# Causal mask by 43 more contraction rows in the diagonal tiles, with the steps reordered

## The chip, the core and the metric

The kernel runs on one core of a Trainium2 chip. The core has five engines that run their own instruction streams: TensorE (PE, whose weight loads are listed apart as PEld), VectorE (DVE), ScalarE (ACT), GpSimd (POOL) and SyncE (SP), which here only issues DMAs. Sixteen DMA engines move the data; one DMA instruction is cut into packets that some of these engines carry. Engines wait for each other by semaphores; a DMA adds 16 to its semaphore in all. The metric is the device time of one execution in microseconds, as the median of several runs.

## The reference

Eight sequences of 512 tokens with 128 features go through layer norm, a gated linear attention with 8 heads and two decay states each, a sign-weight feed-forward layer, a causal attention with 16 heads of 8 features (rotary positions), and the same feed-forward layer again, each with a residual. All work on the change lies in the causal attention:

```
qkv = layernorm(x) @ qkv_w.T + qkv_b ; q, k get rotary positions      # 16 heads of 8
scores[q, k] = q . k / sqrt(8), for k <= q only
ctx = softmax(scores) @ v ; x = x + ctx @ proj_w.T + proj_b
```

## The kernel before

**Stages.** For each sequence b there are five stages: norm (letter n), scan (s, the linear attention), mid (m, the feed-forward and the projections for q, k, v), maxima (x) and attn (a). Each engine has its own generator for each stage, which yields between steps, and a string of letters for each engine (`PE_ORDER`, `ACT_ORDER`, `DVE_ORDER`, `POOL_ORDER`, `SP_ORDER`, lines 86 to 127) says whose next step comes. `interleave` walks through the string when the program is built, so each engine's instruction stream is fixed and in order: where one instruction waits, all behind it wait. Different sequences overlap: scan of sequence b+1 stands among maxima and attn of b.

**Operands of the attention.** Sixteen heads are handled in two sets of eight; f = 2b or 2b+1 counts the 16 sets. The queries and keys are each written as a sum of three bf16 parts (`parts`). SP writes the six part tiles of a sequence to DRAM (`scratch`, line 452: 128 rows of 1 KB each, the "spill"), waits until all six have landed (line 457), and then reads them back stacked, so that one contraction over 72 rows gives all nine products of parts (line 463). One such stack is five DMAs for `qs` and three for `ks`: four of 24 rows, two of 16 and two of 8, each row 8 KB. There are three places (`RING`) for stacks.

**Maxima** (PE line 1021): for each head and each of four query tiles of 128, scores against all keys up to and including the tile's own, 128 to 512 columns in one matmul over 72 rows, and then a second matmul (line 1023) of the bf16 identity with a tile of zeros and -3e38 that adds the mask on the 128 columns of the tile's own keys. Two tiles of heads by queries fill one PSUM bank of 512 columns, at 1, 1, 2 or 4 heads a group, 22 groups a set; DVE reduces a bank to row maxima (line 1491). Until the last sequence there is one bank for it. The negated maxima go in three bf16 parts, turned over by PE (line 1029) and copied by ACT (`mT`, line 749), by three small DMAs (line 472) into rows 72 to 74 of `qs`; rows 72 to 74 of `ks` are ones, written once by three DMAs at the start (line 435).

**Attention** (PE line 1051): the transposed scores, keys by queries, over 75 rows, so that the maximum is already subtracted; again a second matmul (line 1053) adds the mask on the diagonal tile. ACT takes the exponent of a bank (line 762), PE multiplies with the values (line 1066). Per set and head there are four tiles with a mask in each of the two passes, so there are 512 mask matmuls at each of the lines 1023 and 1053.

**SP's order.** It begins `nnmmmmmmmm`: after the loads at the start, the load of x for sequence 1, that for sequence 2 (line 425, which waits until the normalised x of sequence 1 has been taken), then the six spills of sequence 0 and its two stacks.

Of the kernel before, what the change touches and what calls it, by code (L numbers as in the profile page):

```python
# [15 lines left out]
P = 128  # L16
# [48 lines left out]
N_STACK = 16 * (len(Q_COPIES) + len(K_COPIES))  # L65
# [26 lines left out]
    "aaxsamaxasamaaxaasasaaamaaxasxaaamaxsaxaaxasaxsasxaxasxaxaaaxasxmaxsxamxsaaaaxsmxaasxaaaxsaaxsxasxsasxsa"
    "xssmxsaxsxasxasxsxasxassxaasxsxaassxsaxaaaxsaaxsxaasxasxaaaxaamxasaxaaaxmasaxaaxaaxsaxaaasxaamxaxaasxama"
    "xaaxsaxsxaxasxasaxsxaasxasxaaxasasxaaxaasxmaxassaxmaxasxsmxasxsasxsaxmxsaxsxaxasaxsaxasxaaxasasaxssaxsxa"
    "sxsaxsaxaaasaxsaaxssaaamasxamxsxaaxaaxaaxaaaxsaaxsxaxaamxasxaaaxaaxasxaaaxsaaxmxaxsassaxaaxaaxasxaasxamx"
    "amsxassaxsmaxsxasxsaxsxsaxasaxsxmxssxaaxssaxssxaaasxasaxasxsxaasxssaaxaasasaxassxaamaxamxaaaxaaaxaaaxamx"
# [4 lines left out]
ACT_ORDER = (
    "nssssssssssssssssssssssssssssmmsnmsmssssssssmsssssssssssmmsssssmmmmssssnssssssssmssssssssssssmsssssxasaa"
    "assmaamsanaamaaamsmmaaamsasssaaasasasxsassassasassaasamaaaasaaaaaasaasaaaamaaaamsssssxamasmasasaamamaaaa"
    "sanaaasmaaaaaaaxssasaasaaaasaasmsasaassasaassssaasaaaasaaasamasamaxsssssmasssanaaamaamaamsaaaaasmaaaaasa"
    "sxaasasamaassaaaassasaasassaasassmasmaaaaaasaasamaamasxsssssamassaasmaaaaaaasnaaaaaaasamaaaxaaasasaaasaa"
    "samsaasasasassssssaasaasaaaaasamasaamxsasmssmsasaaaamaasaamsasanaaasaaaaamaxsaaaaassaaaasasamaassaaasasa"
    "aasasassaaasassaamasxmsamssasmaassssmamaasaaasasaaaaasaxaaamaaaaaaaaaamaaaaaaaaaaaaamamaaaaamaxamaaaaama"
    "maaaaaaaaaaaaaaaxaaaaaaaaaaaaaaaaaaaaaaaaaaaxaaaaaaaaaaaaaaaaaaaaxaaaaaaaaaaaaaaaaaaaaaaaaaaaaaaaaa"
)
DVE_ORDER = (  # L110
    "nnnnssssmsssssnnnnsmsssssssmssmsmsssssmssssssssmssssssssssssssmmmmmmsssssmmsmmmsmmnssssnmnmsnsmsssssssmm"
    "mmsmmmsmmssmsmsssssssssssssssxsssxxssxsxsxsxsxsxxmxmxsxmsmsmxsxmsmxmxsxxsssxmssxssxmssxxxxmnmxssxssssxmx"
    "nmxnmnmxssxsxssxssxsmxmxsmsxsmxmxmmxmxmsxmmxssxsmxmxsxmxmxsxsssmmsmsmxxxsmmxnsnmxsnnxmxsxsxxmmxmmxssxxxs"
    "ssxxsaxamxaasxasaxmxaxxaxxmssmxmaxaxsasxsmasxssaxsaxmxmsxsxmsxssxmsxmxsxxsssxsxxxmsxmxmxxxsxmmsmxmmxssxm"
    "sxsxsmxnmsxsxxxnxmxnssnxsmxsxsmmmxxxsxxsxaamxaxxaxxsmxssasxssaxasaxxmxsxmssxssxssxaxaaxassxamxamxssxsmsx"
    "msxsmmxmxssssxxxsxxsxmsmmmmmmmssmsxmsmxsxmxsmxmsxnxmmxxxnsnxsxnxsxsmxmxsmxmxmxmsxxasaxxaxxxasssaxsssaxsa"
    "xaxmsxmaxaxssxssssxsxaaaxasxmsxsssxmxmxssxssxssxxxxxxmxxsmmsmsxmxmmxmmxxssmxsxsxsxnmsxsxxmxxmxsxssmxsxmn"
    "mxsnxxnxxxxsxsaamaaxmaxammaxasxsmsxmsxssaxaxamxaamxsxaxmsxssxssssxmxmsxxxsssxssssxxxsxsxsxsxmsxsmxmxmsmx"
    "xmxmxmxsmsxsxsxsmmxxsxxsxmxmxmmmxxsxxxxxssaasaxamxasamaxasmmxmxaxmsxaxssxmsxsasaxsamsxmxaxmxsmsxsssxssxx"
    "sxsxssssxxsxxsxssssxxmxmmmxmmxmxxmmxmmxxmxmxxmmmxxxxxmxmxmxmxxxaxxamaaxaaxaaxmxmxaxmxaxaaaxmxaxmxmxxxxxx"  # L120
    "xxxxxxxxxxxxxxxxxxxxxxxxxxxxxxxxxxxaaxaaxaaxaaxxxxxaxaxaaxaxxaxxxxxxxxxxxxaaaaaaaaaaaaaa"
)
POOL_ORDER = (
    "nnssssnsssssssnmnmsssmsxsssssnnssssmnssssmsnssmnsxsmnssmsssmnnsssasssxmnmssmnssnsssssassxmnmsmsssnsnssss"
    "assxmnmssmssssnassssnxsmmnssmsssnsasxssssmmmaxaa"
)
SP_ORDER = "nnmmmmmmmmnxmmmmmmmxnmxmmmammmmxnmmxmmammmmxnmmmxmmmmamxmnxmammmmmmxmmxmmmmammxmxmmmmmmamxmxxaa"
# [16 lines left out]
def hybrid_block(nc, x, weights, vectors, consts, consts_bf, ones, scratch, out):  # L144
    with ExitStack() as ctx:
# [101 lines left out]
        xk = sb("xk", [P, 2, C, D])  # L247
        cT = pT[:, 0, 0:T]
# [10 lines left out]
        ones_in = sem("ones_in")  # L259
# [83 lines left out]

        max_step = sem("max_step")
# [28 lines left out]
        ident = cst[:, C_ID:C_ID + P]  # L373
        tri = cst[:, C_TRI:C_TRI + P]
# [3 lines left out]
        future_qk = cbf[:, P:2 * P]  # L378
# [37 lines left out]

        parts_dram = scratch.rearrange("h p d t -> (h p d t)").rearrange(
# [5 lines left out]
        def _(sp):  # L423
# [10 lines left out]
            for place in range(RING):  # L434
                sp.dma_start(ks[K_MAX:K_ALL, place, :, :], ones[:, 0:HH, :]).then_inc(ones_in, 16)
# [8 lines left out]
            def mid(b):  # L444
                for part, ready in enumerate((part0, part1, part2)):
                    for side in range(2):
                        yield
                        sp.wait_ge(ready, b * 2 + side + 1)
                        if part == 0 and side == 0 and b > 0:
                            for f in (2 * b - 2, 2 * b - 1):  # L450
                                sp.wait_ge(stacked[f % RING], (f // RING + 1) * N_STACK)
                        sp.dma_start(parts_dram[side, part].rearrange("d h t -> (d h) t"),
                                     parts[:, part, side, :]).then_inc(spilled, 16)
                for f in (2 * b, 2 * b + 1):
                    yield
                    if f == 2 * b:
                        sp.wait_ge(spilled, b * 96 + 96)
                    if f >= RING:
                        sp.wait_ge(sc_ps, (f - RING + 1) * 2 * NE)
                    heads = slice(HH * (f % 2), HH * (f % 2) + HH)  # L460
                    for side, (dst, copies) in enumerate(((qs, Q_COPIES), (ks, K_COPIES))):
                        for row, part, n in copies:
                            sp.dma_start(dst[row:row + n * DA, f % RING, :, :],
                                         parts_dram[side, part:part + n, :, heads].rearrange("p d h t -> (p d) h t")
                                         ).then_inc(stacked[f % RING], 16)

            def maxima(b):
                for f in (2 * b, 2 * b + 1):
# [116 lines left out]
        def _(act):  # L585
# [157 lines left out]
            def maxima(b):  # L743
                for f in (2 * b, 2 * b + 1):
# [40 lines left out]
        def _(pe):  # L785
# [210 lines left out]
            def maxima(b):  # L996
                banks = max_banks(b)
                for f in (2 * b, 2 * b + 1):
                    for n, (qt, h0, m) in enumerate(MAX_GROUPS):
                        yield  # L1000
                        if n == 0:
                            if f == 0:
                                pe.wait_ge(masks_in, 16)
# [29 lines left out]
            def attn(b):  # L1033
                def scores(n):
# [39 lines left out]
                if b == 0:  # L1074
                    pe.wait_ge(masks_in, 16)
                    pe.wait_ge(ones_in, 16 * RING)
# [35 lines left out]
        def _(dve):  # L1112
# [371 lines left out]
            def maxima(b):  # L1484
                s = Steps(max_step, b * MAX_STEPS)
# [110 lines left out]
```

## Time and profile before

| | us |
|---|---|
| median of 3 runs | 749.57 |
| lowest and highest run | 744.65, 756.94 |
| the profiled execution, its own time | 753.01 |
| span from first to last instruction in it | 750.9 |
| mean granted TensorE clock in it | 0.941 of full |

Engine times in the profile are busy times. A matmul's time is modelled from its start to its end and includes the passage through the array, so that neighbours overlap: what a matmul takes from the stream of PE is the distance to the next start. The chain of waits is followed back from the last instruction; its pieces add up to the span. Where a view names a queue (SPq), it is the engine's issuing side.

### The profile page before, as it was taken

How to read it: one execution, taken by the hardware profiler on the slowest of the kernel's cores; microseconds unless marked ns; L12 is line 12 of the kernel's file. 1: busy time of each engine (PE TensorE's matmuls, PEld its weight loads, DVE VectorE, ACT ScalarE, POOL GpSimd, SP SyncE). 2: the span in 40 equal slices, each digit the busy share in tenths (PEclk: the TensorE clock that was granted, in tenths of full speed). 3: DMA queues.
4: the chain of work that ended last, by engine and by line, in shares of the span. 5: the costliest groups of instructions: out<-in, count | busy, mean ns of one | idle time of the engine just before them, and what ended most of it. 6: DMA issues, size and time to landing. Idle time of an engine off the chain costs nothing.

```text
span 750.9 us, 17433 instructions
## 1 busy us (share of the span) xinstructions
PE 653.8 (87%) x6640; PEld 375.3 (50%) x6670; DVE 563.3 (75%) x1571; ACT 426.4 (57%) x900; POOL 187.8 (25%) x231
## 2 busy tenths in 40 slices
PE   3666767889999999999999999999999998899885
PEld 2334435445554655555646554556555545356333
DVE  4675673788976988899888879896899678768302
ACT  2543642545686558746775568465866563563750
POOL 4241640244043313422134212241243110100000
PEclk9689896599999999999999999999999999999985
DMA  3000026000450044002700161014301340540000
GB/s 107 1 1 1 16 69 101 2 17 2 87 100 1 17 98 89 2 10 66 113 17 24 52 99 29 2 58 76 55 9 56 63 64 17 96 75 3 16 1 14
DMA packets 20934, 32.37 MB, mean 43 GB/s; under 512 B 3178, under 2 KB 18282, under 8 KB 18538
## 3 DMA queue, kind: packets, MB, share of 16 engines
q1 hardware_dynamic: 20850, 31.25, 21.2%
q8 instruction: 53, 0.87, 0.5%
q14 instruction: 31, 0.25, 0.1%
HBM read 22.46 MB, written 8.39 MB: 41 GB/s over the span
## 4 chain that ended last, share of the span: by engine, by line
PE 55%; DVE 24%; issue 8%; ACT 7%; DMA 3%; POOL 2%; SPq 1%; DVEq 0%; ACTq 0%; POOLq 0%
PE ps L1066 8%; PE ps L1021 8%; PE ps L1051 8%; DVE mrow L1491 7%; PE ps L795 5%; PE ps L869 3%; DVE qkf L1460 3%; PE ps L896 3%; PE ps L1053 3%; DVE am L1335 3%; PE ps L1023 2%; PE ps L790 2%; PE ps L916 2%; ACT pT L762 2%; PE ps L905 2%
## 5 line engine op out<-in xcount | busy, mean ns | idle before, releaser
L1491 DVE TENSOR_REDUCE mrow<-ps 128x1 f32<-128x384 f32 (+3 forms) x352 | 221.4, 634 | 78.5 <-PE ps L1023 76.0
L762 ACT ACTIVATE pT<-ps 128x512 f32<-128x512 f32 (+1 forms) x352 | 186.9, 558 | 105.1 <-PE ps L1053 101.6
L1021 PE MATMUL ps<-ks,qs 72*128 72x512 bf16 (+3 forms) x512 | 140.0, 309 | 17.3 <-DVE mrow L1491 14.1
L1051 PE MATMUL ps<-qs,ks 75*128 75x256 bf16 (+3 forms) x512 | 131.5, 305 | 4.1 <-DMA qs<-mT 2.5
L1023 PE MATMUL ps<-cbf 128*128 128x128 bf16 x512 | 101.5, 224 | 0.0
L1066 PE MATMUL ps<-pT,va 128*32 128x512 f32 (+3 forms) x1024 | 96.1, 451 | 5.3 <-ACT pT L762 5.0
L1021 PEld LDWEIGHTS ps<-ks,qs 72*128 72x128 bf16 x512 | 50.3, 99 | 96.0 <-DVE mrow L1491 78.2
L1053 PE MATMUL ps<-cbf 128*128 128x128 bf16 x512 | 98.0, 221 | 0.0
L546 POOL TENSOR_TENSOR spread<-state,cst 128x144 f32<-128x144 f32 x112 | 47.5, 445 | 186.8 <-DVE state L1364 153.2
L1051 PEld LDWEIGHTS ps<-qs,ks 75*128 75x128 bf16 x512 | 50.5, 99 | 76.0 <-ACT pT L762 30.6
L534 POOL TENSOR_TENSOR xe<-lpart,hot 96x1024 bf16<-96x1024 bf16 x32 | 60.3, 1893 | 47.8 <-DVE lpart L1321 47.8
L503 POOL TENSOR_TENSOR mid_rstd<-mid_ve,half 128x4 f32<-128x4 f32 x24 | 26.0, 1083 | 156.6 <-DVE mid_ve L1148 156.6
L639 ACT ACTIVATE dec<-ps 128x512 f32<-128x512 f32 x64 | 38.4, 600 | 47.0 <-PE ps L858 46.7
L629 ACT ACTIVATE qM<-qT,cst 128x256 f32<-128x256 f32 x128 | 53.5, 497 | 0.0
L1023 PEld LDWEIGHTS ps<-cbf 128*128 128x128 bf16 x512 | 51.3, 100 | 4.4 <-issue 2.4
L1053 PEld LDWEIGHTS ps<-cbf 128*128 128x128 bf16 x512 | 50.6, 99 | 1.9 <-issue 0.7
L1335 DVE TENSOR_TENSOR am<-dec,ps 128x1024 f32<-128x1024 f32 x32 | 38.9, 1215 | 16.5 <-PE ps L869 16.4
L503 POOL TENSOR_TENSOR attn_rstd<-attn_ve,half 128x4 f32<-128x4 f32 x8 | 8.5, 1057 | 134.1 <-DVE attn_ve L1148 134.1
L698 ACT ACTIVATE yT<-ps,epsc 128x512 f32<-128x512 f32 x32 | 21.9, 685 | 30.0 <-PE ps L896 30.0
L869 PE MATMUL ps<-qM,kT 128*64 128x512 f32 x128 | 38.4, 666 | 0.0
L1066 PEld LDWEIGHTS ps<-pT,va 128*32 128x32 f32 x1024 | 20.6, 108 | 32.9 <-ACT pT L762 15.6
L896 PE MATMUL ps<-am,vg 128*32 128x128 f32 x1024 | 35.3, 279 | 0.5 <-DVE ytmp L1378 0.5
(189 smaller groups left out, 1092.6 us busy)
## 6 DMA issues: line engine op xcount, KB each, us to landing
ks<-scratch SPq DMA_DIRECT2D x48, 192.0 KB
scratch<-parts SPq DMA_DIRECT2D x48, 128.0 KB, 1.7
qs<-scratch SPq DMA_DIRECT2D x32, 128.0 KB
qs<-scratch SPq DMA_DIRECT2D x16, 192.0 KB
x<-x SPq DMA_DIRECT2D x8, 256.0 KB, 3.1
qs<-scratch SPq DMA_DIRECT2D x32, 64.0 KB
out<-xk SPq DMA_DIRECT2D x8, 256.0 KB, 2.4
qs<-mT SPq DMA_DIRECT2D x48, 8.0 KB
```

The costliest lines, as they stand in the source:

```text
L534: pool.tensor_tensor(xe[rows, c % 2, :, :], lpart[rows, c, :].unsqueeze(1).broadcast_to([PARTS * QUAD, HJ, LB]), hot[rows, :].unsqueeze(2) ...
L629: ins = act.activation(qM[:, h, :], qT[:, cp * 2 * P:(cp + 1) * 2 * P], ACT.Copy, scale=headmask[:, h:h + 1])
L762: act.activation(pT[:, c0:c0 + m, P_OFF[kt]:P_OFF[kt] + width], ps[:, score_banks(b)[n % len(score_banks(b))], 0:m * width].rearrange("p ( ...
L869: mm = pe.matmul(ps[LB * q:LB * q + LB, BK_G, :], kT[:, at:at + LB], qM[:, :, at - (c // 2) * 2 * P:at - (c // 2) * 2 * P + LB], start=Tru ...
L896: mm = pe.matmul(o[:, :, LB * q:LB * q + LB], v_columns(c, q, 4 * g + i), am[:, c % 2, 4 * g + i, :, :], start=True, stop=True, skip_group ...
L1021: pe.matmul(o, qs[0:K_MAX, f % RING, h, qt * P:(qt + 1) * P], ks[0:K_MAX, f % RING, h, 0:width], start=True, stop=False, skip_group_check= ...
L1023: mm = pe.matmul(o[:, qt * P:(qt + 1) * P], ident_bf, future_qk, start=False, stop=True, skip_group_check=True)
L1051: pe.matmul(o, ks[0:K_ALL, place, h, kt * P:(kt + 1) * P], qs[0:K_ALL, place, h, kt * P:T], start=True, stop=False, skip_group_check=True)
L1053: mm = pe.matmul(o[:, 0:P], ident_bf, future_kq, start=False, stop=True, skip_group_check=True)
L1066: mm = pe.matmul(ps[q:q + QUAD, BK_PV, kt * P:T], va_columns(b, kt, 4 * g + i), pT[:, i, P_OFF[kt]:P_OFF[kt] + T - kt * P], start=(kt == 0 ...
L1335: dve.tensor_tensor(am[:, c % 2, :, :, :], dec[:, c % 2, :, :].rearrange("p (h j) t -> p h j t", j=J), gq.unsqueeze(2).broadcast_to([P, H, ...
L1491: dve.tensor_reduce(mrow[:, qt, h0:h0 + m], ps[:, max_banks(b)[n % len(max_banks(b))], 0:m * width].rearrange("p (m k) -> p m k", k=width) ...
```

## The change

In place of the mask matmul, the diagonal tile gets more rows of contraction. `MARKS` is (128 + 2) // 3 = 43, and rows 75 to 117 of both `qs` and `ks` hold marks, three tokens to a row with three weights of different size (2^-39, 2^12, 2^63), such that their products add a large negative number exactly where the key is later than the query. The diagonal 128 columns are now a matmul of their own over 118 rows; the columns before (or, in attn, after) them are another over 72 (or 75) rows, where there are any. In the first query tile of maxima and in the last key tile of attn nothing but the diagonal is left, so one matmul stands where there were two.

The marks are made once: six small DVE instructions (a first step of maxima in DVE's order), two PE transposes, one ACT copy that writes `marks` on 43 partitions, and six DMAs on SP, for `qs` and `ks` of each of the three places, of 43 rows, in which the 1 KB of a row is written for each of the 8 heads. SP's order now begins `nnxmmmmmmmm`: the six DMAs stand between the load of x for sequence 2 and the spills of sequence 0. As the diagonal matmul of maxima now runs over rows 72 to 74 too, each stack has a ninth DMA that writes zeros to these rows of `qs`. The order strings of all five engines are new; PE's has the first scores of maxima after 81 steps of scan and 12 of mid, as before, and PE, ACT, DVE and SP have one step of maxima more.

```diff
-N_STACK = 16 * (len(Q_COPIES) + len(K_COPIES))
+N_STACK = 16 * (len(Q_COPIES) + len(K_COPIES) + 1)
+MARKS = (P + 2) // 3
+K_DIAG = K_ALL + MARKS
+MARK = (2.0 ** -39, 2.0 ** 12, 2.0 ** 63)
...
-SP_ORDER = "nnmmmmmmmmnxmmmmmmmxnmxmmmammmmxnmmxmmammmmxnmmmxmmmmamxmnxmammmmmmxmmxmmmmammxmxmmmmmmamxmxxaa"
+SP_ORDER = "nnxmmmmmmmmnxmmmmmmmxnmmmxmmammmxnmmxammmmmxmnxmmmmammmxnmmxmmmmmamxmmxmmmmammxmmmmxmmmmaxmxaxa"
...
+        marks_tok = pT[:, 2, 0:MARKS].bitcast(BF16).rearrange("p (s r) -> p s r", s=2)
+        marks = pT[0:MARKS, 3, 0:T].bitcast(BF16).rearrange("p (s t) -> p s t", s=2)
...
+        zeros = consts_bf[0:1, 2 * P:3 * P].unsqueeze(1).broadcast_to([PARTS, HH * C, P])
...
+                    sp.dma_start(qs[K_MAX:K_ALL, f % RING, :, :].rearrange("p h (c t) -> p (h c) t", t=P), zeros
+                                 ).then_inc(stacked[f % RING], 16)
             def maxima(b):      # SP
+                if b == 0:
+                    yield
+                    sp.wait_ge(marks_ready, 1)
+                    for place in range(RING):
+                        for side, dst in enumerate((qs, ks)):
+                            sp.dma_start(dst[K_ALL:K_DIAG, place, :, :],
+                                         marks[:, side, :].unsqueeze(1).broadcast_to([MARKS, HH, T])
+                                         ).then_inc(marks_in[place], 16)
...
             def maxima(b):      # PE
+                if b == 0:
+                    yield
+                    pe.wait_ge(masks_in, 16)
+                    pe.wait_ge(marks_step, 6)
+                    for side in range(2):
+                        mm = pe.transpose(ps[0:MARKS, BK_MAX, :].bitcast(BF16)[:, side * P:(side + 1) * P],
+                                          marks_tok[:, side, :], ident_bf)
+                    mm.then_inc(marks_ps, 1)
...
-                            pe.matmul(o, qs[0:K_MAX, f % RING, h, qt * P:(qt + 1) * P], ks[0:K_MAX, f % RING, h, 0:width],
-                                      start=True, stop=False, skip_group_check=True)
-                            mm = pe.matmul(o[:, qt * P:(qt + 1) * P], ident_bf, future_qk,
-                                           start=False, stop=True, skip_group_check=True)
+                            own_tile = slice(qt * P, (qt + 1) * P)
+                            if qt > 0:
+                                pe.matmul(o[:, 0:qt * P], qs[0:K_MAX, f % RING, h, own_tile],
+                                          ks[0:K_MAX, f % RING, h, 0:qt * P], start=True, stop=True, skip_group_check=True)
+                            mm = pe.matmul(o[:, own_tile], qs[0:K_DIAG, f % RING, h, own_tile],
+                                           ks[0:K_DIAG, f % RING, h, own_tile], start=True, stop=True, skip_group_check=True)
...
-                        pe.matmul(o, ks[0:K_ALL, place, h, kt * P:(kt + 1) * P], qs[0:K_ALL, place, h, kt * P:T],
-                                  start=True, stop=False, skip_group_check=True)
-                        mm = pe.matmul(o[:, 0:P], ident_bf, future_kq, start=False, stop=True, skip_group_check=True)
+                        own_tile = slice(kt * P, (kt + 1) * P)
+                        mm = pe.matmul(o[:, 0:P], ks[0:K_DIAG, place, h, own_tile], qs[0:K_DIAG, place, h, own_tile],
+                                       start=True, stop=True, skip_group_check=True)
+                        if kt + 1 < C:
+                            mm = pe.matmul(o[:, P:width], ks[0:K_ALL, place, h, own_tile], qs[0:K_ALL, place, h, (kt + 1) * P:T],
+                                           start=True, stop=True, skip_group_check=True)
```

## Rows read from the trace of the kernel before

**Rows 1.** The page, engine totals of the whole span

```profile
PE 653.8 (87%) x6640; PEld 375.3 (50%) x6670; DVE 563.3 (75%) x1571; ACT 426.4 (57%) x900; POOL 187.8 (25%) x231
```

**Rows 2.** Stretches: length, busy us of each engine (count), clock, DMA share, GB/s

```profile
525.00:575.00 50.00, 48.07 (x491) 28.34 (x490) 45.49 (x126) 34.69 (x78) 15.30 (x15) 1.00 0.17 30
```

**Rows 3.** The chain of waits, whole span: share by line

```profile
by line: PE ps L1066 8.4%; issue 7.7%; PE ps L1021 7.6%; PE ps L1051 7.5%; DVE mrow L1491 6.7%; PE ps L795 5.1%; PE ps L869 3.3%; DVE qkf L1460 2.9%; PE ps L896 2.7%; PE ps L1053 2.5%; DVE am L1335 2.5%; PE ps L1023 2.4%; PE ps L790 2.2%; P
```

**Rows 4.** The DMA view: packets, the queue, issues with KB and us to landing

```profile
q1 hardware_dynamic: 20850, 31.25, 21.2%
...
ks<-scratch SPq DMA_DIRECT2D x48, 192.0 KB
scratch<-parts SPq DMA_DIRECT2D x48, 128.0 KB, 1.7
qs<-scratch SPq DMA_DIRECT2D x32, 128.0 KB
qs<-scratch SPq DMA_DIRECT2D x16, 192.0 KB
x<-x SPq DMA_DIRECT2D x8, 256.0 KB, 3.1
qs<-scratch SPq DMA_DIRECT2D x32, 64.0 KB
out<-xk SPq DMA_DIRECT2D x8, 256.0 KB, 2.4
qs<-mT SPq DMA_DIRECT2D x48, 8.0 KB
...
cst<-consts SPq DMA_DIRECT2D x1, 220.0 KB, 3.0
...
ks<-ones SPq DMA_DIRECT2D x3, 24.0 KB
```

**Rows 5.** Two groups of instructions: count, then busy us and mean ns

```profile
L762 ACT ACTIVATE pT<-ps 128x512 f32<-128x512 f32 (+1 forms) x352 | 186.9, 558 | 105.1 <-PE ps L1053 101.6
...
L1023 PE MATMUL ps<-cbf 128*128 128x128 bf16 x512 | 101.5, 224 | 0.0
```

**Rows 6.** The chain in order of time, after a wait: start, us, what

```profile
211.55 0.23 PE ps L1021
211.78 0.06 PE ps L1023
```

**Rows 7.** Waits, whole span: who waited for whom: us in total, times, longest

```profile
ACT pT L762 <- PE ps L1053: 101.6, 115, 4.1
...
DVE mrow L1491 <- PE ps L1023: 76.0, 112, 3.6
```

**Rows 8.** SP in order of time: start, us of issuing, DMA, count

```profile
78.80 0.40 SPq L425 DMA_DIRECT2D x<-x  x1
100.52 6.68 SPq L452 DMA_DIRECT2D scratch<-parts  x6
108.59 1.75 SPq L463 DMA_DIRECT2D qs<-scratch  x5
```

**Rows 9.** The chain in order of time, at the third stack

```profile
201.67 9.83 DMA ks<-scratch
```

**Rows 10.** Stretches with only spills (first) or only mT rows (second)

```profile
101.00:102.50 1.50, 1.30 (x14) 1.03 (x10) 1.47 (x3) 0.27 (x1) 0.00 (x0) 1.00 0.25 87
629.00:632.50 3.50, 2.66 (x27) 1.92 (x27) 3.23 (x8) 0.52 (x1) 0.00 (x0) 1.00 0.05 12
```

**Rows 11.** The chain, an mT row just behind a stack, and one later

```profile
363.75 4.18 DMA qs<-mT
...
661.03 1.92 DMA qs<-mT
```

**Rows 12.** SP in order of time, the third stack

```profile
199.06 1.75 SPq L463 DMA_DIRECT2D qs<-scratch  x5
```

**Rows 13.** PE in order of time, first score matmul of the kernel

```profile
122.23 0.31 PE L1021 MATMUL ps<-ks,qs 72*128 72x128 bf16 x1
```

More of the change, by code:

```diff
@@ L92 @@
[L92 to L96, printed above, removed]
@@ new lines @@
+    "axaaxasaaaxaasaxssxsmaxaaxsaaxssxaaaxamxaasxaaasxaaxaasxaassaxaaxassxaasxaaxamaaxsaxmsxasxasxsxamsaxsxax"
+    "saxmaxsaaxssaxssaxsxasxsxaaaxasxaaaxsxaaxsaxsaaxasxmaaxmxsxaxaasaaxsxaaxaaaaaxasaaxmaaxasxasaxaxmxaassxx"
+    "saaxaasxasxasaxaaaxssaasxsxaaaxmaaxmxasxsasxsxassxmxasxsxasxsxsaxsxssxsxsxasxaasaxasxamaxaaasxasaaxasaxa"
+    "axsaaaxsmxasmaxaaasaasaaamxaaaasaxamxasxaaxasaxaxaaxssxsxaaxasaxsxaamxsaaxmaasaxamxaaxaasxaaxssxasxsasxs"
+    "axssxmaxssxasxaxssaxsaxssxasaxsxaasxasxsaaxasaxasxaaxssxaaaxaaaxmasaxaxaamaaxsaxasxaaaxaaaxasaxaxaasxama"
@@ new lines @@
+    "xaaaxssxaaxmxssaxaxaasxsxasxaxaasaxaaxamsxaaxassaxmaxsaxmsxasssaxssxaxmxsaxsxaxasaxsaxsaasxaxassxasasxaa"
+    "axssxsxaxaasaaaxsaxassaaaxmasamxaxasxsxaaaxaaaxsaxaxaaxamaxasxaaaxaaxasaxaxasaxmxaxsaassxaaxaaaxsaxasaxm"
+    "saxmsxaxassmxasxassxsasxaaxassxmxxaxssxaasxsxsaaxasaxssxassxaaxssxsaaaxaasasaxassxaamaxamaxaaxaaaxaaaxaa"
+    "xaxaaxamaxaxmxaaxaaaaxaxaaxaxamaaxmxaaxaaxaaxamaxaxxaxaxmxaxxaxxaxaaxaxaaxaxaaxaaxaxaaxaaxaaxaaxaxaaaxaa"
+    "aaxxaaaaaxaxxaxaaaxaxxaxaxaaxxxaaaaaaxaxxxxaaaxaaxxaaaaxaaxxaaxxxaxxaxaaxxxxaaaxaaaxaxxxaaaaxxaxaaxaxaaa"
@@ L100 @@
+    "aaxaaaaaaaaaaaaaaaaaaaaaaaaaaaaaaaaaaaaaaaaaaaaaaaaaa"
 )
 ACT_ORDER = (
[L102 to L105, printed above, removed]
@@ new lines @@
+    "aaasaaaaamsaaaaaxssasaasaaaasasasaasamssassaasssaasaaaasaamasaaamasxsssssassmsaanaamamaaamaasaaaaasmaaax"
+    "saasaassaamaasasaassasaasaasssassamasaamaaaasaaaaasasmnmxsssssaamsaassamaaaaasaaaaaaaaasmaaaxasaaasaaaas"
+    "saaasasamsasassassasssaaaasaaamaaasamsxsmsasssasamaaasamaaamssaaaaaasaaanaamxaasaaassaaaassaaaamassaasas"
+    "aaasaasssasaasasaamasxmsmassmasaassassmmaaasasasaaaaaaasaxaamaaaaaaaaaaaaaamaaaaaaaamaamaaaaaamxammmaaaa"
+    "aaaaaaaaaaaaaaaaxaaaaaaaaaaaaaaaaaaaaaaaaaaaaxaaaaaaaaaaaaaaaaaaaaxaaaaaaaaaaaaaaaaaaaaaaaaaaaaaaaaa"
@@ L116 @@
[L116 to L120, printed above, removed]
@@ L121 @@
-    "xxxxxxxxxxxxxxxxxxxxxxxxxxxxxxxxxxxaaxaaxaaxaaxxxxxaxaxaaxaxxaxxxxxxxxxxxxaaaaaaaaaaaaaa"
+    "nnnnsxsssmsssssnsnnsnmmsssssmssssmsssmsssssssssssmsssssssssssssmmmmmmsssssmmsmmmsmmnssssnmnsnmssmssssssm"
+    "msmmmsmmsmmsmsmsssssssssssssssxsssxxssxsxsxsmxsxsxxmxxsxmsmxsmsmxsmxmxsxxsssxsssxsxxxmsxmmxsnmxsssxsssxm"
+    "xsnmxmnmxxnsssxsssxsmxmxmsxssxmxsmxmmxmmmsxmxssxmxssmsxssmxxmxxmxsmsmxxxmsxsxnsxnmnmnxsxxmxsmxxmxmmsmsxx"
+    "sxsssxsaxamxasaxmaxamxaxxaxsxmmxmasxsxasasxasasxsmxaxsxmxmsxsxsmsxsmxsxsxxsssxsxxxmxmxsxmxmxxssmmxmxmsms"
@@ new lines @@
+    "sxmsxsxnxsnxsnmnxxmxxmxsmxsmsmxsxsxsxxsxxmxaaxxaxxaxmssxsasxassxsxaaxsxmmxssxssxssxaxasaxasamxaxmmxsssxs"
+    "mmmxmxssxxssssxxxxsxsxsmmmmmmmmssmsxmsmxsxmxsxsxmxmxmmxxnxnsxnsxnsxsxmmxsmxmxxmxmxasaxxaxxaxsssasxsasxsm"
+    "asxaxmxsaxasasxsasxssxamxaxmxsmxsssxssxssxxsxssxsxxxxxxxmmssmsmxxmmxmxmxssxsxsxsnxsxmsxmmxxmxmxsmxnmsxsm"
+    "xsxxnxsxxxxxsaansmaxamaxammmaxassxssxssxaxaxmaxamaxsxaxsssxssxssmxmmxmxssxxsssxsssxxxxsxsxssxmxmxssxmmsx"
+    "mmxxmxssxsxsxsxxmmxmmsxsxxmxmxmsmxmxsxxxxxsaasaxamxasamaxasmxmmxamxssxasxmxsasaxsaxsmxaxsmxsmmxssxssxssx"
@@ L258, in hybrid_block @@
         x_in = sem("x_in")
-        ones_in = sem("ones_in")
+        ones_in = [sem("ones_in%d" % place) for place in range(RING)]
         cleared = sem("cleared")
@@ L341, in hybrid_block @@
         stacked = [sem("stacked%d" % place) for place in range(RING)]
+        marks_ps = sem("marks_ps")
+        marks_step = sem("marks_step")
+        marks_ready = sem("marks_ready")
+        marks_in = [sem("marks_in%d" % place) for place in range(RING)]
         max_step = sem("max_step")
@@ L373, in hybrid_block @@
         ident = cst[:, C_ID:C_ID + P]
+        after = cst[:, C_AFTER:C_AFTER + P]
         tri = cst[:, C_TRI:C_TRI + P]
@@ L434, in _ @@
             for place in range(RING):
-                sp.dma_start(ks[K_MAX:K_ALL, place, :, :], ones[:, 0:HH, :]).then_inc(ones_in, 16)
+                sp.dma_start(ks[K_MAX:K_ALL, place, :, :], ones[:, 0:HH, :]).then_inc(ones_in[place], 16)
             def norm(b):
@@ L743, in maxima @@
             def maxima(b):
+                if b == 0:
+                    yield
+                    act.wait_ge(marks_ps, 1)
+                    act.activation(marks.rearrange("p s (c t) -> p s c t", c=C),
+                                   ps[0:MARKS, BK_MAX, :].bitcast(BF16)[:, 0:2 * P].rearrange("p (s t) -> p s t", s=2)
+                                   .unsqueeze(2).broadcast_to([MARKS, 2, C, P]), ACT.Copy).then_inc(marks_ready, 1)
                 for f in (2 * b, 2 * b + 1):
@@ L756, in attn @@
                         width = T - kt * P
+                        if n == 0 and b == 0:
+                            for place in range(RING):
+                                act.wait_ge(marks_in[place], 32)
                         if g >= 1:
@@ L997, in maxima @@
                 banks = max_banks(b)
+                if b == 0:
+                    yield
+                    pe.wait_ge(masks_in, 16)
[4 more added lines that the diff above has]
+                    mm.then_inc(marks_ps, 1)
                 for f in (2 * b, 2 * b + 1):
@@ L1002, in maxima @@
                             if f == 0:
-                                pe.wait_ge(masks_in, 16)
+                                pe.wait_ge(marks_ready, 1)
+                            if f < RING:
+                                pe.wait_ge(marks_in[f], 32)
+                                pe.wait_ge(ones_in[f], 16)
                             pe.wait_ge(stacked[f % RING], (f // RING + 1) * N_STACK)
@@ L1484, in maxima @@
             def maxima(b):
+                if b == 0:
+                    yield
+                    dve.wait_ge(consts_in, 16)
+                    for k in range(3):
+                        n = len(range(k, P, 3))
+                        for side, (table, mark) in enumerate(((ident, -MARK[2 - k]), (after, MARK[k]))):
+                            to, columns = marks_tok[:, side, 0:n], table[:, k:P:3]
+                            if k == 0:
+                                ins = dve.tensor_scalar(to, columns, mark, None, ALU.mult)
+                            else:
+                                dve.wait_ge(marks_step, 2 * k)
+                                ins = dve.scalar_tensor_tensor(to, columns, mark, to, ALU.mult, ALU.add)
+                            ins.then_inc(marks_step, 1)
                 s = Steps(max_step, b * MAX_STEPS)
```

31 lines of the change are left out of this document (9 added, 22 removed).

## The prediction

> **What bounds the kernel now.** First the engine totals [rows 1]: PE is busy 87% of the span and DVE 75%. In a stretch of the steady part [rows 2] both are nearly full, PE 48.07 and DVE 45.49 of 50 us, at full clock. So neither has much room, but PE's number is modelled and counts overlapping matmuls twice, so the next view is the chain of waits by line [rows 3]: the lines of score matmuls, values, masks and reduces share it, and no single one holds it. The two mask lines have 2.5% and 2.4%. Last come the DMA rows, because the change adds DMAs in SP's queue ahead of the spills: nothing there looks tight by share, 21.2% of the 16 engines [rows 4], but a share says nothing about one of the sixteen.
>
> **The masks that go.** There are 512 at each of the two lines, listed at 224 ns [rows 5]. What one takes from PE's stream is less: in the chain, the step from a mask to the next start is 0.06 us [rows 6]. All 1024 are thus 61 us of stream. The columns of the diagonal are not computed twice any more, and splitting the score matmul adds no columns; 256 tiles need one matmul less. How much of 61 us is on the path? By the chain, 4.9% of 750.9 is 36.8 us, about 600 of the 1024. From below: DVE waited for a mask 112 times and ACT 115 times [rows 7]; a group has 512/352 = 1.45 masks (22 groups for 32 tiles in each set), so at least 227 x 1.45 x 0.06 = 20 us stand directly ahead of a wait that would end sooner. Where two chains tie, the second takes over when the first is shortened, so the chain's number is too good; I take the middle of 20 and 37, **28 us less**, with 20 and 61 for the range. PE's new order has its steps in all but the same sequence, so I add nothing for the reordering.
>
> **The making of the marks.** Eight small instructions and one ACT copy of 1024 columns: twice the 558 ns of a 512-column one [rows 5] is 1.1 us. They sit where scan of the first sequences runs; between nothing and 3 us, I take 1.
>
> **The zeros.** A ninth issue on SP for each of 16 stacks, 1.75/5 = 0.35 us [rows 8], and 96 packets of 256 B. Only where a stack is late does it count; the chain shows one such long wait [rows 9]. Between 0 and 16 x 2 us; I take 1.
>
> **The six marks DMAs, the term that decides.** How many DMA engines carry a DMA can be read from a count of packets. By the shapes in [rows 4], if each contiguous run is one packet, q1 should hold: 48 spills x 128; 16 loads and stores of x x 512 runs of 512 B; stack rows of 8 KB 64 x 24 + 32 x 16 + 32 x 8; 48 mT x 8; six loads of 128 rows at the start (the one of the constants stands for them); three of ones x 3. That is 6144 + 8192 + 2304 + 384 + 768 + 9 = 17801. The queue has 20850 [rows 4], 3049 more. These must be the semaphore writes, one for each engine that takes part. If a DMA of 128 or 16 rows uses 16 engines, of 24 rows 12, of 8 rows 8 and of 3 rows 3, that is 102 x 16 + 64 x 12 + 80 x 8 + 9 = 3049, to the last one. With 16 engines for 24 rows it would be 3305, with 8 it would be 2793. So the number of engines is the largest divisor of the rows that is not over 16. **43 is prime: one engine.** All six DMAs have 43 rows, so all six go to one and the same engine, 6 x 43 x 8 = 2064 packets of 1 KB (the source is 1 KB a row, repeated for each head).
>
> The Trainium skill, DMA: Bandwidth & Descriptors, section "Why a DMA increments its semaphore by 16 and not by 1", states the same: the slowest dimension decides, 127 partitions go to 1 engine, and on this kind of queue it is the lowest-numbered ones. The trace's 3049 agrees; that 43 rows go to one, no row here shows.
>
> The rate of one engine: where only spills run, 87 GB/s at a share of 0.25 [rows 10] is 87/4 = 21.8 GB/s per engine, 47 ns for 1 KB. Where only mT rows run, also from SBUF to SBUF, 12 GB/s at 0.05 is 15 GB/s, 68 ns, but there eight engines read the same few partitions; the marks have one engine alone, so I take 47 and keep 68. Then 2064 x 0.047 = 97 us, against 12 in which sixteen engines would hardly be noticed (97/16 = 6).
>
> When: SP issues x for sequence 2 at 78.80, landed 3.1 us later [rows 4, 8], and by the new order the marks come directly behind, from 81.9 to 178.9. The spills of sequence 0 are issued at 100.52 [rows 8], but the same queue's packets on that engine are served in turn: an mT DMA just behind a stack took 4.18 us in the chain, one elsewhere 1.92 [rows 11]. Each spill has 8 packets there; 48 x 0.047 = 2.3, so the last lands at 181.2. SP then issues the stack; the third stack took from 199.06 [rows 12] to 201.67 + 9.83 = 211.50 [rows 9], 12.4 us. First scores: 193.6. Before, they started at 122.23 [rows 13] with the stack issued at 108.59 [rows 8], landing by 12.4 us at 121.0, just in time. PE stands still from there, and scan of the next sequences with it, since its steps are behind in PE's one stream; DVE and ACT run dry. **71 us more** (at 68 ns: 2064 x 0.021 = 43 more, 115).
>
> **Sum.** 753.0 - 28 + 1 + 1 + 71 = 798 for an execution like the profiled one, which was 3.4 above the median of the three runs; against the median 749.6: **795 us**. Its own range: with the whole 61 of masks saved 762, with 20 saved 803, with slower packets 838.
>
> **Rivals.** *The marks spread out* (some even split of the rows, such as eleven engines): all land well before the spills, at 97/11 = 9 us from 82; what is left is 749.6 - 28 + 2 = **724**, faster. Against it is the exact count above; for it, that no DMA of an odd number of rows above 3 is in the trace. It decides as soon as the marks land before about 107, where the spills have been issued: that is, from four engines on (82 + 24 = 106). The change is then what it says. *Spread out, and DVE takes PE's place*: DVE is at 91% [rows 2]; if only the waits of DVE itself shorten, 112 x 1.45 x 0.06 = 10 us, **742**, no change. *One engine, and slow packets* as for mT: **838**. *The stall is shorter*, because the spill's packets on that engine are served in between and not behind: then the marks of the first place, 688 packets, bind, 82 + 32 = 114, and there is no stall; this falls in with 724 and [rows 11] speak against it.
>
> **Chances.** One engine at 47 ns, 0.74; slow packets 0.08; 724 with either cause 0.12; 742 0.06. A difference of 2% (15 us) is about what a measurement of this kernel can tell from none. Slower 0.82, within 2% 0.06, faster 0.12. The range 740 to 840 takes in the forecast with its own bounds and the DVE rival; the 724 rival and the slowest packets stay out.
>
> **What would show it.** In the profile after: between about 125 and 180 us PE, DVE and ACT idle and the DMA share at 0.06 (one of sixteen) at 22 GB/s; the first score matmul at 190 or later; the six spills with tens of us to landing, and SP waiting for them; 6 more semaphore writes for the marks in q1, not 96. If the first score matmul stands near 122, the forecast is wrong at the engine count; if it stands at 150 to 170, at the rate. For the masks: the two mask lines gone, PE's matmuls 6640 less about 256, and the time from the first score matmul to the end, now 750.9 - 122.2 = 628.7, at about 601.

## The result, and the profile after

The changed kernel took 806.12 us as the median of 4 runs (802.89 to 810.43); the kernel before took 749.80 beside it. The ratio is 1.078 [1.070, 1.086], so it is slower by 56 us. The profiled execution took 806.41 us, its span is 804.3 us. Forecast were 798 for such an execution and 795 against the median, in a range of 740 to 840. Here and below a ratio is taken over the executions within 1.5% of the fastest of their kernel, so it can differ from that of the medians, above all where it leaves out many: it stands on 2 of 4 executions for e2_four_on_one, 3 of 12 for e3_no_masks, 3 of 6 for e9_no_masks_new and 8 of 12 for e10_zeros_first.

First the engine totals and the queue row of the page after; they answer to [rows 1, 4].

```profile
span 804.3 us, 16989 instructions
...
PE 618.2 (77%) x6416; PEld 355.3 (44%) x6416; DVE 560.1 (70%) x1577; ACT 424.8 (53%) x901; POOL 190.9 (24%) x231
...
q1 hardware_dynamic: 24504, 33.76, 21.0%
```

PE has 35.6 us less of busy time and 224 matmuls less (256 tiles need one less; some records can be missing). DVE has six instructions more and about the same time. So less work, in more time: something is idle. The slices of the page say where. Each digit is 20.1 us.

```profile
PE   3667861003789799989898999999999898788885
...
DVE  5856650001899779877997998889699977857502
ACT  2544630000555775668466756866595665364651
...
PEclk9796785555799899999999999999999999899966
DMA  2000000027000520251037004400530341170000
```

From the seventh slice to the tenth PE is nearly empty; DVE is empty in the seventh to the ninth, and ACT up to the tenth. The granted clock is at 0.5, its lower level (1.2 GHz), while PE stands still, and from the first score matmul to the end it is 0.94, against 0.96 before. In two stretches inside that hole (columns as in [rows 2]):

```profile
140.00:160.00 20.00, 0.00 (x0) 0.00 (x0) 0.00 (x0) 0.00 (x0) 0.00 (x0) 0.50 0.07 24
170.00:175.00 5.00, 0.00 (x0) 0.00 (x0) 0.00 (x0) 0.00 (x0) 0.00 (x0) 0.50 0.50 167
```

Nothing runs but DMA at a share of 0.07, hardly more than one engine of sixteen (0.0625), at 24 GB/s. Then, at 170, the share jumps to 0.50: these are the spills. SP's queue shows what was issued when (start, us from the first issue to the end of the last, engine line, out<-in, count); L491 are the marks, L468 the spills, L479 and L482 the stacks.

```profile
78.73 0.40 SPq L441 DMA_DIRECT2D x<-x  x1
85.39 0.81 SPq L491 DMA_DIRECT2D qs<-pT  x1
86.25 10.66 SPq L491 DMA_DIRECT2D ks<-pT  x1
96.96 15.12 SPq L491 DMA_DIRECT2D qs<-pT  x1
112.11 14.76 SPq L491 DMA_DIRECT2D ks<-pT  x1
126.92 14.89 SPq L491 DMA_DIRECT2D qs<-pT  x1
141.85 14.89 SPq L491 DMA_DIRECT2D ks<-pT  x1
156.78 17.30 SPq L468 DMA_DIRECT2D scratch<-parts  x6
179.19 1.75 SPq L479 DMA_DIRECT2D qs<-scratch  x5
180.97 1.19 SPq L479 DMA_DIRECT2D ks<-scratch  x3
182.21 0.28 SPq L482 DMA_DIRECT2D qs<-consts_bf  x1
```

Before, the first spill was issued at 100.52 and the first stack at 108.59 [rows 8]. Here SP itself is held: the *issue* of the second marks DMA takes 10.66 us, and from the third on it takes about 14.9 us for 344 packets, 43 ns each. That is the pace of one engine: 24 GB/s in the stretch above is 43 ns for 1 KB too. So the spills were not only late to land; five of them were not even issued before 171. The chain of waits goes through the same place (start us, us, what), and PE's timeline and its waits (us in total, times, longest) show where it ends:

```profile
156.78 14.85 SPq L468
...
173.63 5.54 DMA scratch<-parts
...
182.21 10.76 DMA qs<-consts_bf
...
193.10 0.59 PE ps L1071 x4
```

```profile
123.96 1.09 PE L825 MATMUL ps<-cst,xn 128*128 128x128 f32 x4 [1.11 <-DVE ytmp L1426]
193.10 0.59 PE L1071 MATMUL ps<-ks,qs 118*128 118x128 bf16 x4 [68.05 <-DMA qs<-consts_bf]
```

```profile
PE ps L1071 <- DMA qs<-consts_bf: 75.2, 5, 68.0
```

The first score matmul starts at 193.10, against 122.23 in [rows 13]: 70.9 us later. From it to the end there are 611.2 us, against 628.7: 17.5 less. 70.9 - 17.5 = 53.4, and 753.0 + 53.4 = 806.4, the whole difference of the two profiled executions.

### The profile page after: what moved, and what is told of

It reads as the page before. It is cut to its first block, busy times and chain, and to the rows that moved or that the text cites. A ratio compares the mean times of both kernels' runs of the same rounds, so it can differ in the third digit from the quotient of the medians.

```text
span 804.3 us, 16989 instructions
## 1 busy us (share of the span) xinstructions
PE 618.2 (77%) x6416; PEld 355.3 (44%) x6416; DVE 560.1 (70%) x1577; ACT 424.8 (53%) x901; POOL 190.9 (24%) x231
## 3 DMA queue, kind: packets, MB, share of 16 engines
q1 hardware_dynamic: 24504, 33.76, 21.0%
## 4 chain that ended last, share of the span: by engine, by line
PE 42%; DVE 22%; SPq 13%; DMA 8%; ACT 8%; issue 6%; POOL 1%; DVEq 0%; ACTq 0%; POOLq 0%
SPq L491 9%; PE ps L1117 7%; DVE mrow L1552 6%; PE ps L830 5%; DMA qs<-consts_bf 5%; PE ps L1069 4%; PE ps L1100 3%; PE ps L1103 3%; ACT pT L797 3%; PE ps L1071 2%; DVE qkf L1508 2%; PE ps L904 2%; SPq L468 2%; DVE am L1383 2%; PE ps L825 2%
## 5 line engine op out<-in xcount | busy, mean ns | idle before, releaser
L1071 PE MATMUL ps<-ks,qs 118*128 118x128 bf16 x512 | 92.4, 227 | 77.0 <-DMA qs<-consts_bf 75.2
L1069 PE MATMUL ps<-ks,qs 72*128 72x128 bf16 (+2 forms) x384 | 100.2, 283 | 26.4 <-DVE mrow L1552 25.2
L1117 PE MATMUL ps<-pT,va 128*32 128x512 f32 (+3 forms) x1024 | 99.1, 464 | 7.8 <-ACT pT L797 7.6
L1103 PE MATMUL ps<-qs,ks 75*128 75x256 bf16 (+2 forms) x384 | 98.1, 287 | 0.0
L1100 PE MATMUL ps<-qs,ks 118*128 118x128 bf16 x512 | 91.9, 229 | 4.5 <-ACT pT L797 2.4
L1071 PEld LDWEIGHTS ps<-ks,qs 118*128 118x128 bf16 x512 | 47.6, 101 | 87.8 <-issue 74.2
L1100 PEld LDWEIGHTS ps<-qs,ks 118*128 118x128 bf16 x512 | 46.6, 101 | 71.9 <-ACT pT L797 34.9
L1069 PEld LDWEIGHTS ps<-ks,qs 72*128 72x128 bf16 x384 | 37.0, 98 | 91.6 <-DVE mrow L1552 83.9
L634 ACT ACTIVATE gex<-gin 128x128 f32<-128x128 f32 x8 | 2.4, 304 | 77.9 <-DVE gin L1310 77.9
L1103 PEld LDWEIGHTS ps<-qs,ks 75*128 75x128 bf16 x384 | 39.0, 102 | 5.2 <-issue 2.8
```

The source lines that it names most:

```text
L1069: pe.matmul(o[:, 0:qt * P], qs[0:K_MAX, f % RING, h, own_tile], ks[0:K_MAX, f % RING, h, 0:qt * P], start=True, stop=True, skip_group_chec ...
L1071: mm = pe.matmul(o[:, own_tile], qs[0:K_DIAG, f % RING, h, own_tile], ks[0:K_DIAG, f % RING, h, own_tile], start=True, stop=True, skip_gro ...
L1100: mm = pe.matmul(o[:, 0:P], ks[0:K_DIAG, place, h, own_tile], qs[0:K_DIAG, place, h, own_tile], start=True, stop=True, skip_group_check=True)
L1103: mm = pe.matmul(o[:, P:width], ks[0:K_ALL, place, h, own_tile], qs[0:K_ALL, place, h, (kt + 1) * P:T], start=True, stop=True, skip_group_ ...
L1117: mm = pe.matmul(ps[q:q + QUAD, BK_PV, kt * P:T], va_columns(b, kt, 4 * g + i), pT[:, i, P_OFF[kt]:P_OFF[kt] + T - kt * P], start=(kt == 0 ...
```

## The experiments

The theory: the six marks DMAs of 43 rows go to one DMA engine, and all behind them waits. The first rival: the number of engines doesn't matter, the amount of data or the place in the queue does. For the masks: their going saves about 28 us wherever the steps stand; the rival is that the saving depends on the order, or doesn't reach the end at all. Ratios are to the kernel before, timed beside each run on the same chip.

**e1_split, e1_again: the same marks, cut so that 42 rows and one row go apart.** The same bytes and the same place in SP's queue; the waits for the marks count 64 in place of 32.

```diff
-                            sp.dma_start(dst[K_ALL:K_DIAG, place, :, :],
...
+                            for r0, r1 in ((0, 42), (42, 43)):
+                                sp.dma_start(dst[K_ALL + r0:K_ALL + r1, place, :, :],
+                                             marks[r0:r1, side, :].unsqueeze(1).broadcast_to([r1 - r0, HH, T])
...
```

> The changed kernel with each marks DMA cut into one of 42 rows and one of 1 row: the same bytes and packets, only on more DMA engines (42 rows divide by 14). Theory A (one engine carried all 2064 packets, and the spills waited behind them): the stall of 68 us before the first score matmul is gone, the first score matmul stands at 125 to 128 us instead of 193.1, and the time is 806 - 68 = 738 (732 to 744), below the kernel before. SP issues each marks DMA in under 1.5 us instead of 15. Rival B (the loss comes from the bytes, 2.1 MB of marks at any spread, or from the spill and the new SP order): the first score matmul stays at 170 or later and the time at 780 or more.

735.87 us, 0.980 [0.976, 0.984]; a second time, on another chip, 735.12, 0.980 [0.976, 0.984]. SP's queue in its profile:

```profile
96.73 2.62 SPq L492 DMA_DIRECT2D ks<-pT  x2
99.58 7.61 SPq L468 DMA_DIRECT2D scratch<-parts  x6
108.59 1.75 SPq L479 DMA_DIRECT2D qs<-scratch  x5
```

The last marks are issued by 99.4, and the stack at 108.59, to the hundredth as before the change. The first score matmul starts here:

```profile
123.03 0.63 PE L1072 MATMUL ps<-ks,qs 118*128 118x128 bf16 x4
```

733.8 - 123.0 = 610.8 us remain after it, and 611.2 in the kernel after. So the two differ in time by the hole and by nothing else that shows; other executions leave 609.3 (e1_again) and 601.9 (e2_four_on_one) behind it. q1 has 24630 packets, 126 more than the 24504 of the kernel after. That is 6 x 21: 22 engines' writes for a pair, less the 1 of before. By the rule it is 14 engines for 42 rows and 8 for the single row, whose next dimension is the 8 heads; the count shows only their sum.

**e2_four_on_one: only the third place cut**, so that four of the six marks DMAs stay on one engine. The edit against e1_split:

```diff
-                            for r0, r1 in ((0, 42), (42, 43)):
+                            for r0, r1 in (((0, 42), (42, 43)) if place == 2 else ((0, 43),)):
```

> As e1_split, but only the two marks DMAs of the third place are cut into 42 and 1 rows; the four of the first two places stay at 43 rows. A dose for theory A: 4 x 344 packets on one engine. In the changed kernel SP needed 14.9 us for each marks DMA and the stack was issued 22.4 us after the last one was done issuing; with four, that is at 126.9 + 22.4 = 149.3, and 13.9 us later, at 163, the first score matmul stands. That is 38 us after the 125 at which PE is ready: 736 + 38 = 774 (766 to 782). If the one engine were not the cause, the time would stay near e1_split's 736.

781.57 us (four executions, 769.88 to 783.09), 1.031 [1.022, 1.040]. The profile is of the shortest of them. The issues, the first score matmul, and PE's waits for the stacks:

```profile
84.85 10.66 SPq L492 DMA_DIRECT2D ks<-pT  x1
95.55 15.12 SPq L492 DMA_DIRECT2D qs<-pT  x1
110.72 14.76 SPq L492 DMA_DIRECT2D ks<-pT  x1
125.52 16.66 SPq L492 DMA_DIRECT2D qs<-pT  x2
142.22 3.30 SPq L492 DMA_DIRECT2D ks<-pT  x2
145.56 4.12 SPq L468 DMA_DIRECT2D scratch<-parts  x6
152.60 1.75 SPq L479 DMA_DIRECT2D qs<-scratch  x5
```

```profile
165.92 0.59 PE L1072 MATMUL ps<-ks,qs 118*128 118x128 bf16 x4 [42.41 <-DMA qs<-consts_bf]
```

```profile
PE ps L1072 <- DMA qs<-consts_bf: 46.2, 4, 42.4
```

Zero, four and six such DMAs give first stacks at 108.59, 152.60 and 179.19, and ratios of 0.980, 1.031 and 1.078. The stack moves by 11 and then by 13 us for each DMA. The first score matmul stands at 123.03, 165.92 and 193.10, so 42.9 and 70.1 us later than with none, and the medians are 735.87, 781.57 and 806.12, so 45.7 and 70.3 more. That is a dose and its response, at the same bytes: the engine count is shown as the cause.

**e3_no_masks: the kernel before without the mask matmuls, all else kept.**

```diff
-                            mm = pe.matmul(o[:, qt * P:(qt + 1) * P], ident_bf, future_qk,
-                                           start=False, stop=True, skip_group_check=True)
...
-                        mm = pe.matmul(o[:, 0:P], ident_bf, future_kq, start=False, stop=True, skip_group_check=True)
```

> The kernel before with its 1024 mask matmuls left out and nothing else (the causal mask is missing from the result). It measures what the removal can be worth in the old order. Theory A (the masks lie on PE's path by about the share of the chain): 37 us less or more exactly 750 - 28 = 722 (713 to 730). Theory C (DVE and ACT take PE's place, only the masks directly ahead of a wait count): 750 - 20 = 730 or above, up to 740.

The ratio is 1.002 [0.997, 1.007], from three executions of 747.76 to 754.21 us; the median of all twelve is 764.18. By either number there is no gain, where my reasoning said 28 us. That fell. The next runs cross the two parts.

**e5_old_orders: e1_split with the order strings of before** (and the four added steps put in where the new strings have them). **e6_new_orders: the kernel before with the new strings** (without those steps). **e9_no_masks_new: e3_no_masks with the new strings.**

```diff
-PE_ORDER = (the new string)
+PE_ORDER = (the old string, with one "x" at place 48)
```

> As e1_split, but with the order strings of the kernel before, with only the four added steps put in at the places where the new strings have them. If the reordering is worth nothing (as forecast), it is within 4 us of e1_split. If the new orders lose something (which would explain why the part behind the stall became shorter by 17.5 us and not 28), it is 5 to 12 us below e1_split; if the new orders gain, it is above.

> The kernel before, mask matmuls and all, with the new order strings (without the four added steps). Orders alone. If they are worth nothing: 750 within 4 us. If they were fitted to the shorter diagonal tiles and suit the old ones less: 752 to 762. If they are better by themselves: under 745.

> The kernel before without its mask matmuls (no causal mask in the result) in the new orders, so without marks, zeros and split matmuls. Against e6_new_orders (753) it prices the masks in these orders; against e1_split (736) it prices marks, zeros and splitting. Theory F (removal is worth about 20 us where the orders allow it, and the marks and zeros cost 3): 733 (728 to 737). Rival G (PE with still fewer columns falls to half clock more often, as in e3_no_masks, where half clock lasted 172 us against 91): 745 or more, with more than 150 us at half clock.

e5_old_orders: 1.006 [1.002, 1.009]. e6_new_orders: 1.006 [1.003, 1.009]. e9_no_masks_new: 0.983 [0.976, 0.990], from 732.62, 742.76 and 742.99 us; the median of all six is 743.77. Of its two expectations theory F has the ratio (737 us), but the profiled execution, at 756.59 us, had by its mean clock of 0.884 about 175 us at half clock, the sign of rival G; so this corner of the table is the least certain. Put in a table, as ratios to before:

| | old orders | new orders |
|---|---|---|
| mask matmuls | 1 | 1.006 |
| marks, split | 1.006 | 0.980 |
| no mask at all | 1.002 | 0.983 |

Neither part alone gives anything; both together give 2%. Split marks (0.980) are no slower than no mask at all (0.983), so marks, zeros and the split matmuls show no cost in these ratios. With the new orders the marks are worth 0.026 x 749.6 = 20 us (give or take 4), with the old ones nothing. Which of the five strings carries it was not tried. The steps of PE are moved by 12 places at most; SP's string puts some steps of spills ahead of an mT load instead of behind it (`xnmxmmmamm` became `xnmmmxmmam`). What is late next in the old orders is in PE's waits for the stack, here e5_old_orders and then e1_again:

```profile
PE ps L1035 <- DMA qs<-consts_bf: 9.3, 5, 2.4
```

```profile
PE ps L1072 <- DMA qs<-consts_bf: 6.5, 4, 2.2
```

and before it was 0.7 us in all. That is suggestive and too small by itself for 19 us, so I took most of the stacks' cost away.

**e7_old_orders_short, e8_before_short, e11_split_short: only the first three stacks read ks, later ones leave it.** This shortens each later stack by three of its DMAs.

```diff
-                        for row, part, n in copies:
+                        for row, part, n in (copies if side == 0 or f < RING else ()):
```

> e5_old_orders (new matmuls, old orders) with the three key DMAs of a stack left out from the fourth set on (the keys of the first three sets are used again, so the result is another). A stack is half as long. Theory D (in the old orders the time that the masks gave back is waited off at the stacks: 39 us of the chain of e5 are DMA waits behind a stack, against 9.8 before): about half of it comes back, 754 - 15 = 739 (732 to 745). Rival E (it went to DVE or to the clock): 754 to 750, no more than the same cut gives the kernel before.

> The kernel before with the same cut of the stacks, as the control of e7_old_orders_short. The chain has one wait for a stack, 9.8 us. Theory D: 2 to 5 us less, 746 to 748. If stacks matter to any kernel alike: as much less as e7 is below e5.

> e1_split with the three key DMAs of a stack left out from the fourth set on, as in e7_old_orders_short (another result). Theory D says that the new orders had already moved the steps so that stacks are seldom waited for: e1_split's chain has one such wait of 9.1 us, so the cut gives at most 2 to 6 us, 730 to 734, against 16 in the old orders. If the new orders gained by something else, the cut should give about as much as there, 720.

e7_old_orders_short (marks, old orders): 0.986 [0.980, 0.991], which is 0.020 or 15 us below e5_old_orders. e8_before_short (the control, masks, old orders): 0.997 [0.994, 1.000], 2 us. e11_split_short (marks, new orders): 0.975 [0.971, 0.980], 3.5 us; neither is clear of noise. So late stacks cost the kernel with marks about 15 us (give or take 5) in the old orders, and hardly anything in the two others. The chain of e5_old_orders names four places:

```profile
199.97 11.02 DMA qs<-consts_bf
...
274.91 9.07 DMA qs<-consts_bf
...
433.00 9.05 DMA qs<-consts_bf
...
651.83 9.91 DMA qs<-consts_bf
```

39 us on the chain, where the kernel before has one such piece of 9.83 [rows 9]. The first of the four is the third stack, which e7_old_orders_short leaves as long as it is, and its chain has it still (10.52 us); of the three later ones it has none. The sum on the chain alone would not show it, since e1_again has 29.8 us of such pieces at 731.7. My reading is that PE comes to the next stack sooner, since it has no masks to do, but the stack is made from a spill and can't start sooner, and the time saved is waited off. The 15 us are shown for the kernel with marks; for e3_no_masks no such run was made.

**e10_zeros_first: e1_split with the zeros DMA ahead of the eight copies of a stack.**

```diff
+                    sp.dma_start(qs[K_MAX:K_ALL, f % RING, ...], zeros ...
                     for side, (dst, copies) in enumerate(((qs, Q_COPIES), (ks, K_COPIES))):
...
-                    sp.dma_start(qs[K_MAX:K_ALL, f % RING, ...], zeros ...
```

> As e1_split, but each stack's zeros DMA is issued ahead of its eight copies and not behind them. Behind them it adds its own issue and landing to a stack that is waited for (13.8 us from issue to landing in the changed kernel against 12.4 before). If these 1.4 us count, the time is 1 to 4 us below e1_split's 736; if another chain ends at the same time, no difference.

752.1 us, 1.000 [0.996, 1.004]: missed by 17 to 20 us. The place of one DMA of 24 KB among nine is worth the whole gain. PE's waits for the stacks:

```profile
PE ps L1072 <- DMA ks<-scratch: 18.0, 7, 4.3
```

Six pieces of 7.7 to 13.1 us on the chain are now stacks. A stack also takes longer from its first issue to its landing: the first 109.78 to 125.82 (16.0 us) and the third 198.48 to 213.50 (15.0), where the third of e1_again took 13.2. The landings are the ends of these pieces of the chain:

```profile
112.74 13.08 DMA ks<-scratch
...
201.43 12.07 DMA ks<-scratch
```

I had taken the ninth DMA to be harmless wherever it stands.

**e12_zeros_8k: e1_split with the zeros from DRAM**, where heads 8 to 15 of the ones are written as zeros, so that a zeros DMA is 3 packets of 8 KB in place of 96 of 256 B.

```diff
-        zeros = consts_bf[0:1, 2 * P:3 * P].unsqueeze(1).broadcast_to([PARTS, HH * C, P])
+        zeros = ones[:, HH:2 * HH, :]
```

> The marks are split as in e1_split, and the zeros for rows 72 to 74 come from DRAM (the unused heads 8 to 15 of the ones, written as zeros), so that one zeros DMA is 3 packets of 8 KB in place of 96 of 256 B; the same bytes on the same three engines. If it is the number of small packets that lengthens the waited stacks (13.8 us in the kernel after, 12.4 before), the stacks on the chain fall to 9 or below and the time from 736 to about 731. If the bytes or the ninth DMA itself do, or nothing does, it stays at 735 to 737. q1 should then hold 24630 - 1536 + 48 = 23142 packets.

> The same kernel as e1_split, timed beside e12_zeros_8k with more rounds: both theories say 736, ratio 0.98, and it gives the comparison within one chip. A second profile also tells how much its granted clock and its waited stacks vary between executions: if the stack waits on the chain are again one of about 9 us, the count of them belongs to the kernel, otherwise to the execution.

731.22 us, 0.976 [0.972, 0.980], against 735.12 of e1_again on the same chip. q1 holds the 23142 packets expected, and the wait is

```profile
PE ps L1072 <- DMA qs<-ones: 3.6, 3, 1.6
```

The third stack takes from 199.13 to 210.95, 11.8 us, against 195.53 to 208.74, 13.2, in e1_again (one execution of each). The order of the two is as the theory of small packets has it, but the intervals overlap, so I call that likely and not shown; the chain of e12_zeros_8k still has three stack pieces of 8.5 to 9.4 us, where 9 or below was expected. It is the fastest of the kernels here that compute the whole reference. The two profiles of the same kernel, e1_split and e1_again, have one stack piece and three on the chain: their number belongs to the execution as much as to the kernel.

## Why the prediction was right, and where it was not

**The engine count: right, and shown.** "43 is prime: one engine." The packets of q1 after are 24504. The count of [rows 4] was 17801 + 3049; with 6 x 344 marks, 16 x 96 zeros, 6 x 1 semaphore writes for the marks and 16 x 3 for the zeros it is 17801 + 2064 + 1536 + 3049 + 6 + 48 = 24504, to the last one. Six writes, not 96, as forecast. The Trainium skill, DMA: Bandwidth & Descriptors, section "Why a DMA increments its semaphore by 16 and not by 1", says the same of 127 partitions. The trace agrees for 43 rows, and for a pair of 42 rows and of one row with 8 heads it has the sum that the rule gives, 22.

**The stall: the right cause, and a size that owes something to luck.** Forecast was a first score matmul at 193.6 and 71 us more; measured are 193.10 and 70.9. Four terms were off, and cancel. The marks started at 85.39 and not at 81.9, because the ACT copy that makes them came later (3.5 more). A packet took 43 ns and not 47: 2064 x 0.043 = 89 us in place of 97 (8 less). The last spill landed at 179.2, about 5 us behind the marks and not 2.3, and the stack took 13.8 us and not 12.4 (4 more together). The slow-packet rival (68 ns) is ruled out, and so is the one in which the spills are served in between.

**A mechanism that I left out, without loss.** I had the spills issued on time and waiting in one engine's queue. In fact SP was blocked in the issue itself: five of the six spills were issued after 171 and all had landed by 179.2, so the sign "tens of us to landing" did not come. As all that SP has to do next needs the spills, the sum is the same. Had a DMA that doesn't need them stood behind the marks, SP would have issued it late too; no run has one.

**The masks: the step failed, the sum did not show it much.** Forecast was 28 less and the rest after the first score matmul at about 601; measured is 17.5 less and 611. These 10.5 us, less the 2 forecast for the making and the zeros, whose cost is inside the 70.9 and the 17.5, are the 8 by which 806.4 lies above 798. "I add nothing for the reordering" is the failed step, and with it the 28 that were to come whatever the orders. The table above has nothing for the masks in the old orders, and 20 us in the new ones: the new orders are not worth anything by themselves (1.006) but are what lets the saving reach the end. My bounds of 20 and 37 were read from where the masks stand on the chain; neither asked what PE would come to early. It was there in [rows 9], one stack already waited for, and I named it for the zeros alone. I had said that a second chain takes over when the first is shortened, and priced it by the middle of two bounds rather than by its place: the spill, the stack, the maxima.

**The making of the marks** was put at 1 us; the scan step after it starts at 123.96 in place of 121.35, 2.6 us, which the stall covers.

**The zeros** were put at 1 us in all, from an issue of 0.35. The third stack took 12.4 us before and the first took 13.8 after (179.19 to 192.97), which is inside the 70.9. e10_zeros_first shows that this DMA can cost 16 us more when it is put ahead. In the place where the change has it, no run shows clear of noise what it costs: about 4 us for its small packets by e12_zeros_8k, and nothing for marks and zeros together by e9_no_masks_new. The 1 us stays unproven; its range (up to 32) is wide enough for both places.

**What stays open.** In the kernels without mask matmuls the granted clock is lower: in the executions behind the ratios it was 0.902 to 0.929 for e3_no_masks, 0.894 to 0.915 for e9_no_masks_new and 0.917 to 0.941 for e5_old_orders, against 0.931 to 0.974 for the kernel before beside them. The mean clock times the span, about 0.950 x 748 = 711 us before, is 0.915 x 750 = 686 for e3_no_masks: 25 us less, counted at full clock, in the same time. So part of what the masks gave may have been taken back by a lower clock. Against the clock as the whole answer: e7_old_orders_short had 0.917 to 0.946 and e5_old_orders 0.917 to 0.941, yet the first is 15 us shorter; and e1_split took 735.94 us at 0.896 and 735.80 at 0.936. For e3_no_masks itself the question is open: its only profile is of an execution of 763.38 us. Whether PE's waits for the stacks bring the clock down, or whether it fell for another reason and the waits follow, no run here tells apart. Open, too, is which order string lets the saving through. Nor is it settled why the zeros cost 16 us when they stand ahead of the copies; what shows is that the stacks take about 2 us longer. The larger packets were tried behind the copies only.

## What to carry to other kernels

Before a DMA is added, work out how many engines carry it; the packet counts of the queues tell the rule, and by it a prime number of rows above 16, here 43, puts all of it on one engine. Here that also held the queue that issued it. Cutting 43 rows in 42 and 1 turned 7.8% slower into 2% faster. And where a saving of PE time is forecast, ask what PE arrives at early: here it was a transfer made from other engines' results, and the order of the steps and the length of the transfer decided what was left of the saving.

## What the hardware showed that was not expected

- The issue of a DMA was held while the one engine that it and those ahead of it needed was behind. The first marks DMA was issued in 0.81 us, the second in 10.66, each later one in 14.8 to 15.1 and the first spill in 14.85, the time of 344 packets. Cut in 42 rows and one, a pair took 1.75 to 2.8 us (e1_split).
- 1 KB packets from SBUF to SBUF on an engine that has them alone took 43 ns; eight engines with mT rows looked like 68 [rows 10].
- The same nine DMAs of a stack, with the smallest one last: 0.980 of the kernel before; with it first: 1.000.
